# A modulated transformer block on one core: one load moved ahead, gates ahead of LoRA parts, one moment on another engine, two banks traded, two FFN steps reordered

## The chip, the cores and the metric

One core of one Trainium2 chip runs the whole program in one launch. The metric is the device time in microseconds (us); lower is better. The engines are named as in the profile: PE is the tensor engine, DVE the vector engine, ACT the scalar engine, POOL the GpSimd engine, and SPq is the queue of the sync engine, which here issues nearly all DMAs.

## The reference

Two batches of 512 tokens with 512 features go through a block with adaptive layer norm: six modulation vectors (a shift, a scale and a gate for each half) come from `silu(c) @ wmod`.

```python
mod = (_silu(L0_c) @ L0_wmod).reshape(2, 6, 1, -1)
sa, ca, ga, sb, cb, gb = (mod[:, 0], mod[:, 1], mod[:, 2], mod[:, 3], mod[:, 4], mod[:, 5])
ga = (2 * (ga >= 0) - 1) * jnp.maximum(jnp.abs(ga), 0.25)      # gb likewise
h = _layernorm(x) * (1 + ca) + sa
x = x + ga * (h @ (weight * mask_by_32x32_blocks).T + bias)      # first half
h = _layernorm(x) * (1 + cb) + sb
h1 = lora(h, w1, A1, B1); h3 = lora(h, w3, A3, B3)               # hidden width 1376, rank 16, scaling 2
x = x + gb * lora(silu(h1) * h3, w2, A2, B2)                     # the FFN
```

## The kernel before

Every product is computed in about fp32 accuracy with three passes in fp32r: each operand is split in a high part and a low part, and high x high, high x low and low x high are added up in PSUM. ACT mostly makes the high parts (a copy with a cast) and DVE the low parts (source minus high).

There is no scheduler. Each engine runs its own hand-written list of instructions in order, and semaphores tie the lists together. So an instruction that waits holds up all that stands behind it in its engine's list. The same holds for the list of DMAs that SPq issues; they all go over one set of DMA engines.

The first half works as follows. PE builds scale columns from `ca`; the layer norm is folded into the masked weight and four rank-one terms, so that `attend(b, k, m, tiles)` can multiply raw x by scaled weights for batch b, block k of the features and pass m. What the norm still needs comes in by `attend_end(b)`, which multiplies two small tiles: `norm_rows` (the moments of x, turned by PE in `turn_moments(b)`) and `uv_parts` (the masked weight times shift and scale, from `rows_sa`, `columns_sa`, `uv`, `uv_select`, and split by DVE in `uv_split`). The moments of batch 0 are DVE's `moment_a(0, t)` (two instructions, statistics and aggregation), and those of batch 1 are ACT's `row_sum`, `means` and `square_sum`; POOL takes the root of each in `root(i, at)`. The gate `ga` comes from PE `gate_rows(0)`, ACT `gate_abs(0)`, DVE `gates_of(0)`, PE `spread_gate`, and an ACT copy. `turn_moments(0)` may not overwrite the bank `up_b` before `gates_of(0)` has read it (it waits for `gates_ready`).

Then DVE multiplies each tile of batch 0 by gate and norm (`attn_gate`), POOL and DVE add two tiles each to x (`add_x1`), DVE takes the moments of the new x (`moment_f(i)`), POOL takes their roots in two calls of two tiles, ACT and DVE normalize two tiles each (`norm`), and PE turns the result (`turn(q)`, into banks `up_a`, `up_b` and the two side banks); ACT's `high(q)` puts in shift and scale and makes the high part.

The FFN walks over 22 steps s (11 blocks j of the hidden width for each batch): `up(s, 0)` into `up_a`, `up(s, 1)` into `up_b`, then `down(s - 1, t)`. The LoRA terms are merged into the weights while batch 0 runs. A weight comes in three pieces for each j (PIECE numbers them): for a piece, PE `merge(r)` multiplies LoRA parts into a bank, DVE `merge(r)` adds it to the loaded weight, ACT `weight_high(r)` makes its high part and DVE `weight_low(r)` its low part. LoRA tensors themselves come in five cuts, each made into a high part by ACT `lora_high(n)` and completed by DVE `lora_part(n)`; `parts_ready` counts the latter. POOL `spread(j)` makes the small tile b13 for the merges from the first parts. The first two merges use `up_a` and `up_b`, before `turn(0)` and `turn(1)` write there.

Of the kernel before, what the change touches and what calls it, by code (L numbers as in the profile page):

```python
# [9 lines left out]
ACT = mybir.ActivationFunctionType  # L10
# [11 lines left out]
T = S // P  # L22
# [106 lines left out]
def build(nc, x, x_cols, mask, weight, bias, ffn, lora, c, wmod_ca, wmod_sa, wmod, identity, consts, out):  # L129
# [4 lines left out]
    with ExitStack() as ctx:  # L134
# [165 lines left out]
        stats_ready = [sem(f"stats_ready{i}") for i in range(4)]  # L300
        moments_ready = [sem(f"moments_ready{i}") for i in range(4)]
# [84 lines left out]
        def merge_bank(r):  # L386
            return (up_b, up_a)[r] if r < FIRST_MERGES else side[SIDE[("merge", r)] % 2]
# [33 lines left out]
        def _(sp):  # L421

            def load_x(b):
                for t in range(T):
                    sp.dma_start(xt[:, b, t], x_rows[b, :, t]).then_inc(x_loaded[b][t], 16)
# [22 lines left out]
            load_x(0)  # L448
            load_x_chunk(1, 0)
            sp.dma_start(sa_sb[:], wmod_sa).then_inc(sa_loaded, 16)  # L450
            for k in range(1, KT):
                load_x_chunk(1, k)
            load_lora(0)
            load_lora(1)
            load_mod(GATE_A, SHIFT_F, wmod_ga_loaded)
            load_x(1)
# [29 lines left out]
        def _(pool):  # L486
# [6 lines left out]
            def root(i, at):  # L493
# [6 lines left out]
                else:  # L500
                    pool.wait_ge(moments_ready[i], n)
# [76 lines left out]
        def _(act):  # L578
# [57 lines left out]

            def norm_rows_evacuate(b):
# [83 lines left out]
            lora_high(0)  # L721
            lora_high(1)
            gate_abs(0)
            row_sum(0)
            row_sum(1)
            norm_rows_evacuate(0)
            uv_high()
            row_sum(2)

            act.wait_ge(gate_spread, 1)  # L730
            nc.scalar.activation(gate_row_a[0], up_b[:], ACT.Copy).then_inc(gate_copied, 1)
            row_sum(3)
# [3 lines left out]
            mod_evacuate()  # L736
            norm(0)
# [39 lines left out]
        def _(dve):  # L777
# [225 lines left out]
            moment_a(0, 0)  # L1003
            moment_a(0, 1)
            masked_weight_low(1, 1)
            moment_a(0, 2)
            columns_sa()
            moment_a(0, 3)
            masked_weight_low(1, 2)
            norm_parts(0)  # L1010
            uv_sum()
            lora_part(0)
            gates_of(0)
            masked_weight_low(1, 3)
            lora_part(1)
            uv_split()
            nc.vector.tensor_copy(half_on[:], const[:, HALF_ON:HALF_ON + 2]).then_inc(half_on_ready, 1)
# [16 lines left out]
            moment_f(3)  # L1034
            merge(0)
            norm_parts(1)
# [503 lines left out]
```

## Time and profile before

| | us |
|---|---|
| median of 3 runs | 253.34 (253.24 to 253.77) |
| the profiled execution | 253.32 |
| its span in the trace | 251.5 |
| PE busy in the span | 240.4 |
| DVE, ACT, POOL busy | 150.8, 92.4, 41.5 |

The span is that of the engines' instructions; 1.8 us of the profiled execution's time lie outside it. The PE stream is continuous for nearly all of the span, so the table is read by its complement: the span less PE's busy time, 11.1 us, is all that a change in the order of work can touch at all.

### The profile page before, as it was taken

The numbers are of one execution on the slowest core, as the hardware profiler recorded it, in microseconds if no ns is written. First come the engines' busy times: TensorE is split into PE (matmuls) and PEld (weight loads), VectorE is DVE, ScalarE is ACT, GpSimd is POOL, SyncE is SP. The second block draws the span as 40 slices with busy tenths as digits, with TensorE's granted clock in tenths as the row PEclk, the third lists the DMA queues.
The fourth block names the chain that finished last, engine by engine and source line by source line (L and its number), as shares of the span: only waits on it lengthen the run. The fifth ranks groups of instructions, "written<-read, shape, count | busy, mean of one in ns | idle before, by whom it ended". The sixth has DMA issues, their size and how long they took to land.

```text
span 251.5 us, 3419 instructions
## 1 busy us (share of the span) xinstructions
PE 240.4 (96%) x1205; PEld 187.7 (75%) x1205; DVE 150.8 (60%) x260; ACT 92.4 (37%) x168; POOL 41.5 (16%) x57
## 2 busy tenths in 40 slices
PE   7998979799899999999999999999999999999993
PEld 5666546576688888888888878888888888888772
DVE  2769499889886787854654525536453345334524
ACT  2364565673552332375465313112221122122210
POOL 2002367503210130430330100160000000000000
PEclk9999999999999999999999999999999999999999
DMA  5999999322041413133213751040000000000004
GB/s 139 367 389 397 394 402 373 80 86 72 23 175 66 122 46 101 51 102 124 84 44 119 43 42 9 1 167 3 0 1 0 0 3 0 0 0 3 0 0 167
DMA packets 14565, 26.37 MB, mean 105 GB/s; under 512 B 1618, under 2 KB 3538, under 8 KB 14420
## 3 DMA queue, kind: packets, MB, share of 16 engines
q1 hardware_dynamic: 14112, 26.01, 33.2%
q8 instruction: 10, 0.16, 0.3%
q10 hardware_dynamic: 436, 0.15, 0.2%
q14 instruction: 7, 0.06, 0.1%
HBM read 23.26 MB, written 2.10 MB: 101 GB/s over the span
## 4 chain that ended last, share of the span: by engine, by line
PE 77%; DVE 9%; DMA 5%; SPq 4%; issue 3%; POOL 1%; ACT 0%; DVEq 0%; POOLq 0%
PE up_a L1319 16%; PE up_b L1319 15%; PE acc L1345 8%; PE acc L1347 8%; PE acc L1346 8%; PE up_a L1328 8%; PE up_b L1328 7%; DMA sa_sb<-in_wmod_sa 5%; PE side L1301 2%; DVE parts L920 1%; PE acc L1273 1%; DVE wa L933 1%; DVE raw L949 1%; DVE xt L979 1%; PE side L1306 1%
## 5 line engine op out<-in xcount | busy, mean ns | idle before, releaser
L1073 DVE TENSOR_TENSOR g<-up_b,g 128x512 f32<-128x512 f32 (+1 forms) x22 | 15.2, 689 | 43.6 <-PE up_b L1328 43.6
L1345 PE MATMUL acc<-w_hi,g_hi 128*128 128x512 f32 (+1 forms) x88 | 34.9, 396 | 0.0
L1347 PE MATMUL acc<-w_hi,g_lo 128*128 128x512 f32 (+1 forms) x88 | 34.8, 395 | 0.0
L1346 PE MATMUL acc<-w_lo,g_hi 128*128 128x512 f32 (+1 forms) x88 | 34.7, 395 | 0.0
L764 ACT ACTIVATE g_hi<-g 128x512 fp32r<-128x512 f32 (+1 forms) x22 | 13.9, 632 | 54.3 <-DVE g L1073 54.3
L949 DVE SCALAR_TENSOR_TENSOR raw<-side,raw 128x512 f32<-128x512 f32 (+2 forms) x31 | 20.2, 677 | 19.3 <-PE side L1301 11.8
L696 ACT ACTIVATE w_hi<-raw 128x512 fp32r<-128x512 f32 (+2 forms) x33 | 20.3, 626 | 16.0 <-DVE raw L949 16.0
L754 ACT ACTIVATE g<-up_a 128x512 f32<-128x512 f32 (+1 forms) x22 | 13.1, 595 | 32.8 <-PE up_a L1328 32.8
L1319 PE MATMUL up_a<-ht_hi,w_hi 128*128 128x512 f32 (+1 forms) x88 | 24.5, 400 | 0.0
L1319 PE MATMUL up_a<-ht_hi,w_lo 128*128 128x512 f32 (+1 forms) x88 | 23.9, 393 | 0.6 <-DVE w_lo L955 0.6
L1319 PE MATMUL up_b<-ht_hi,w_hi 128*128 128x512 f32 (+1 forms) x88 | 24.0, 394 | 0.0
L1328 PE MATMUL up_b<-ht_lo,w_hi 128*128 128x512 f32 (+1 forms) x88 | 23.8, 392 | 0.0
L1328 PE MATMUL up_a<-ht_lo,w_hi 128*128 128x512 f32 (+1 forms) x88 | 23.8, 392 | 0.0
L1319 PE MATMUL up_b<-ht_hi,w_lo 128*128 128x512 f32 (+1 forms) x88 | 23.7, 391 | 0.0
L955 DVE TENSOR_TENSOR w_lo<-raw,w_hi 128x512 fp32r<-128x512 f32 (+2 forms) x33 | 21.6, 680 | 2.4 <-ACT w_hi L696 0.7
L1077 DVE TENSOR_TENSOR g_lo<-g,g_hi 128x512 fp32r<-128x512 f32 (+1 forms) x22 | 15.1, 688 | 8.6 <-ACT g_hi L764 8.4
L530 POOL TENSOR_SCALAR b<-parts,half_on 128x128 fp32r<-128x128 f32 (+1 forms) x22 | 14.9, 689 | 32.2 <-PE side L1301 19.0
L1319 PEld LDWEIGHTS up_a<-ht_hi,w_lo 128*128 128x128 f32 (+1 forms) x88 | 16.2, 186 | 5.0 <-DVE w_lo L955 1.0
L1345 PEld LDWEIGHTS acc<-w_hi,g_hi 128*128 128x128 f32 (+1 forms) x88 | 16.5, 188 | 4.1 <-issue 0.2
L1347 PEld LDWEIGHTS acc<-w_hi,g_lo 128*128 128x128 f32 (+1 forms) x88 | 16.5, 188 | 4.0
L1346 PEld LDWEIGHTS acc<-w_lo,g_hi 128*128 128x128 f32 (+1 forms) x88 | 16.5, 188 | 3.9
L1319 PEld LDWEIGHTS up_b<-ht_hi,w_lo 128*128 128x128 f32 (+1 forms) x88 | 16.3, 185 | 3.9
(156 smaller groups left out, 339.8 us busy)
## 6 DMA issues: line engine op xcount, KB each, us to landing
raw<-in_ffn SPq DMA_DIRECT2D x33, 256.0 KB, 2.7
xt<-in_x SPq DMA_DIRECT2D x8, 256.0 KB, 9.1
wmod_sb<-in_wmod SPq DMA_DIRECT2D x2, 1024.0 KB, 12.8
wmod_sb<-in_wmod SPq DMA_DIRECT2D x1, 2048.0 KB, 14.7
out<-xt SPq DMA_DIRECT2D x8, 256.0 KB, 2.5
mask_sb<-in_mask SPq DMA_DIRECT2D x4, 256.0 KB, 6.2
ca_sb<-in_wmod_ca SPq DMA_DIRECT2D x4, 256.0 KB, 6.2
wa<-in_weight SPq DMA_DIRECT2D x4, 256.0 KB, 6.4
```

Of the source, the lines that this page charges most:

```text
L530: nc.gpsimd.tensor_scalar(b13[:, n, 0:w], f32(parts[:, LORA_B13 + j * P:LORA_B13 + j * P + w]), half_on[:, n:n + 1], None, ALU.mult).then_ ...
L696: nc.scalar.activation(dst, src, ACT.Copy).then_inc(w_high_ready, 1)
L764: nc.scalar.activation(g_hi[s % 2][0:w], g[0:w], ACT.Copy).then_inc(g_high_ready, 1)
L949: nc.vector.scalar_tensor_tensor(w, merge_bank(r)[0:rows, 0:cols], SCALING, w, ALU.mult, ALU.add).then_inc(merged, 1)
L955: nc.vector.tensor_tensor(low_part, src, f32(high), ALU.subtract).then_inc(w_ready, 1)
L1073: nc.vector.tensor_tensor(g[0:w], up_b[0:w], g[0:w], ALU.mult).then_inc(g_ready, 1)
L1077: nc.vector.tensor_tensor(g_lo[s % 2][0:w], g[0:w], f32(g_hi[s % 2][0:w]), ALU.subtract).then_inc(g_low_ready, 1)
L1319: nc.tensor.matmul(dst[0:w], w_part[j][:, k, n], ht_hi[b][:, k], start=(m == 0 and k == 0), stop=False)
L1328: last = nc.tensor.matmul(dst[0:w], up_hi[j][:, k, n], ht_lo[b][:, k], start=False, stop=(k == KT - 1))
L1345: nc.tensor.matmul(acc[t][:], hi, down_hi[j][0:w], start=(j == 0), stop=False)
L1346: nc.tensor.matmul(acc[t][:], hi, down_lo[j][0:w], start=False, stop=False)
L1347: last = nc.tensor.matmul(acc[t][:], lo, down_hi[j][0:w], start=False, stop=(j == HT - 1))
```

## The change

Nothing of the arithmetic changes but the way in which one tile's mean and variance are computed. In the order of the program:

- SPq: the load of `sa_sb` (1 MB) goes ahead of x tiles 1 to 3 of batch 0; the load of the first gate's weights (`wmod_sb`, 1 MB) goes ahead of two LoRA cuts, and these go between x tiles 1 and 2 of batch 1.
- DVE: `columns_sa` moves behind `moment_a(0, 3)`; `gates_of(0)` and `uv_split` move ahead of `lora_part(0)`. ACT: the two `lora_high` move behind `uv_high` and `norm_rows_evacuate(0)`, which change places, and `row_sum(2)` moves behind the copy of the gate.
- The moments of the last tile of batch 0 after the first half: DVE's `moment_f(3)` goes, ACT's new `moment_last()` comes (a sum, two tiny scalings, a sum of squares), and POOL's root waits for it.
- The first merges trade banks (`up_a` first), each `turn(q)` waits for its own bank's merge alone, PE issues `merge(0)` ahead of the `attend(1, 2, ...)` block, and DVE does `norm_parts(1)` ahead of its `merge(0)`.
- FFN steps 0 and 1 on DVE: `lora_part(2)` goes ahead of everything, `attn_gate(1, 1)` to `(1, 3)` go from between the merges to the ends of steps 0 and 1, `gates_of(1)` goes behind the product of h1 and h3, and `lora_part(4)` goes into the middle piece of step 2.

```diff
@@ def merge_bank
-            return (up_b, up_a)[r] if r < FIRST_MERGES else side[SIDE[("merge", r)] % 2]
+            return (up_a, up_b)[r] if r < FIRST_MERGES else side[SIDE[("merge", r)] % 2]
@@ POOL root
-                    pool.wait_ge(moments_ready[i], n)
+                    if i == NORM_F[0] and n == T:
+
+                        pool.wait_ge(moments_ready[i], T - 1)
+                        pool.wait_ge(last_summed, 4)
+                    else:
+                        pool.wait_ge(moments_ready[i], n)
@@ ACT
+            def moment_last():
+
+                i, t = NORM_F[0], ORDER[T - 1]
+                act.wait_ge(*x1_done(T - 1))
+                act.wait_ge(moments_ready[NORM_A[1]], T + 1)
+                nc.scalar.activation(hbuf[:, 0], xt[:, 0, t], ACT.Copy, accum_out=total[:, 0:1]
+                                     ).then_inc(last_summed, 1)
+                act.wait_ge(last_summed, 1)
+                nc.scalar.activation(total[:, 1:2], total[:, 0:1], ACT.Copy, scale=-D ** -1.5
+                                     ).then_inc(last_summed, 1)
+                nc.scalar.activation(moments[:, i, T - 1, 0:1], total[:, 0:1], ACT.Copy, scale=1.0 / D
+                                     ).then_inc(last_summed, 1)
+                act.wait_ge(last_summed, 3)
+                nc.scalar.activation(hbuf[:, 1], xt[:, 0, t], ACT.Square, bias=total[:, 1:2],
+                                     scale=D ** -0.5, accum_out=moments[:, i, T - 1, 1:2]
+                                     ).then_inc(last_summed, 1)
...
-            lora_high(0)
-            lora_high(1)
             gate_abs(0)
             row_sum(0)
             row_sum(1)
+            uv_high()
             norm_rows_evacuate(0)
-            uv_high()
-            row_sum(2)
+            lora_high(0)
+            lora_high(1)
 
             act.wait_ge(gate_spread, 1)
             nc.scalar.activation(gate_row_a[0], up_b[:], ACT.Copy).then_inc(gate_copied, 1)
+            row_sum(2)
             row_sum(3)
...
             mod_evacuate()
+            moment_last()
             norm(0)
@@ DVE
-            moment_f(3)
+            norm_parts(1)
             merge(0)
-            norm_parts(1)
             norm(0, 2, ORDER[2])
             norm(0, 3, ORDER[3])
             merge(1)
...
-            for i in range(2):
-                attn_gate(1, i)
+            lora_part(2)
+            attn_gate(1, 0)
             for s in range(B * HT):
...
-                if s < 2:
-                    lora_part(2 + s)
+                if s == 1:
+                    lora_part(3)
...
-                if s == 0:
-                    gates_of(1)
-                    for i in range(2, T):
-                        attn_gate(1, i)
-                if s == 2:
-                    lora_part(4)
                 if piece_mid(s):
                     merge(PIECE[piece_mid(s)])
+                    lora_part(4)
                     weight_low(PIECE[piece_mid(s)])
...
+                if s == 0:
+                    gates_of(1)
...
+                if s < 2:
+                    for i in ((1,), (2, 3))[s]:
+                        attn_gate(1, i)
@@ PE
-                if q == 0:
-
-                    pe.wait_ge(merged, FIRST_MERGES)
+                if q < FIRST_MERGES:
+
+                    pe.wait_ge(merged, q + 1)
...
                 if r == 0:
 
+                    pe.wait_ge(uv_ready, 1)
+                elif r == 1:
+
                     pe.wait_ge(cols_ready, 1)
-                elif r == 1:
-
-                    pe.wait_ge(uv_ready, 1)
...
             columns_f()
+            pe.wait_ge(parts_ready, 2)
+            merge(0)
             for m in range(3):
                 attend(1, 2, m, last_two)
-            pe.wait_ge(parts_ready, 2)
-            merge(0)
             attend(1, 3, 0, last_two)
```

The list of DMAs on SPq, from the last of the loads that stay where they were, with what goes and what comes (`xt` is x by tiles, `raw<-in_x_cols` is x of batch 1 by features, `wmod_sb` with 4x512 is the first gate, with 4x1024 the shift and scale of the FFN):

```order
-L425 DMA xt<-in_x 128x512 x4
+L425 DMA xt<-in_x 128x512
 L428 DMA raw<-in_x_cols 128x512
 L450 DMA sa_sb<-in_wmod_sa 128x2048
+L425 DMA xt<-in_x 128x512 x3
 L428 DMA raw<-in_x_cols 128x512 x3
+L437 DMA wmod_sb<-in_wmod 128x4x512
+L425 DMA xt<-in_x 128x512 x2
 L434 DMA lora_raw<-in_lora 128x256
 L434 DMA lora_raw<-in_lora 128x640
-L437 DMA wmod_sb<-in_wmod 128x4x512
-L425 DMA xt<-in_x 128x512 x4
```

The 1 MB of `sa_sb` now has one x tile ahead of it where it had four, and the first gate's 1 MB has none of the LoRA cuts ahead of it; the two x tiles that the piece ends with come behind the cuts.

DVE's list in the first half, before, from `columns_sa` (L861) on; L789 and L791 are a moment, L819 to L826 `norm_parts(0)`, L898 the sum for uv, L920 a `lora_part`, L909 and L912 `gates_of(0)`, L891 the low part of a masked weight:

```order
L861 COPY uv_cols<-up_b 128x4x2 [waits sa_cols_out]
L789 BN_STATS stats<-xt 128x6 [waits moments_ready0,x_loaded0_3]
L791 BN_AGGR moments<-stats 128x2 [waits stats_ready0]
L891 SCALAR_TENSOR_TENSOR wa_lo<-wa,uv_cols,wa_hi 128x512 [waits wa_high_ready1]
L819 SCALAR_TENSOR_TENSOR moments<-moments,rstd 128x4 [waits norm_cols_cleared,rstd_ready0]
L823 CAST norm_cols<-moments 128x4x2x2 [waits deviation_ready]
L826 TENSOR_TENSOR norm_cols<-moments,norm_cols 128x4x2 [waits norm_high_ready]
L898 TENSOR_TENSOR g<-up_a,gate_row 128x512 [waits bias_loaded,uv_out]
L920 SCALAR_TENSOR_TENSOR parts<-parts,const,lora_raw 128x256 [waits const_loaded,parts_high_ready]
L909 TENSOR_SCALAR block_ones<-up_b 128x128 [waits gate_abs_ready]
L912 SCALAR_TENSOR_TENSOR block_ones<-mod_rows,block_ones 128x128 [waits gate_sign_ready]
L891 SCALAR_TENSOR_TENSOR wa_lo<-wa,uv_cols,wa_hi 128x512 [waits wa_high_ready1]
```

The same place in the changed kernel, from the small copy `half_on` on; L888 is now `columns_sa`, L846 to L853 `norm_parts(0)`, L936 and L939 `gates_of(0)`, L918 the low part, L930 `uv_split` and L947 the two `lora_part`:

```order
L1037 COPY half_on<-const 128x2 [waits const_loaded]
L888 COPY uv_cols<-up_b 128x4x2 [waits sa_cols_out]
L846 SCALAR_TENSOR_TENSOR moments<-moments,rstd 128x4 [waits norm_cols_cleared,rstd_ready0]
L850 CAST norm_cols<-moments 128x4x2x2 [waits deviation_ready]
L853 TENSOR_TENSOR norm_cols<-moments,norm_cols 128x4x2 [waits norm_high_ready]
L925 TENSOR_TENSOR g<-up_a,gate_row 128x512 [waits bias_loaded,uv_out]
L936 TENSOR_SCALAR block_ones<-up_b 128x128 [waits gate_abs_ready]
L939 SCALAR_TENSOR_TENSOR block_ones<-mod_rows,block_ones 128x128 [waits gate_sign_ready]
L918 SCALAR_TENSOR_TENSOR wa_lo<-wa,uv_cols,wa_hi 128x512 [waits wa_high_ready1]
L930 SCALAR_TENSOR_TENSOR uv_parts<-uv_parts,const,up_a 128x512 [waits const_loaded,uv_high_ready]
L947 SCALAR_TENSOR_TENSOR parts<-parts,const,lora_raw 128x256 [waits const_loaded,parts_high_ready]
L947 SCALAR_TENSOR_TENSOR parts<-parts,const,lora_raw 128x640 [waits const_loaded,parts_high_ready]
```

The moment that stood behind `columns_sa` is now ahead of it, and the gates stand directly behind the sum for uv, with both LoRA parts at the end.

DVE's list at the start of the FFN, before; L933 is `attn_gate`, L949 `merge`, L920 `lora_part(2)`, L955 `weight_low`, L909 and L912 `gates_of(1)`, L1073 the product of h1 and h3, L1077 its low part:

```order
L933 SCALAR_TENSOR_TENSOR wa<-acc,rstd,mask_sb 128x512 [waits gate_row_loaded0_1,x1_by_pool,rstd_ready2,attn_out] x2
L949 SCALAR_TENSOR_TENSOR raw<-side,raw 128x512 [waits merge_out,raw_loaded2]
L949 SCALAR_TENSOR_TENSOR raw<-side,raw 128x512 [waits merge_out,raw_loaded3]
L920 SCALAR_TENSOR_TENSOR parts<-parts,const,ca_sb 128x1120 [waits const_loaded,parts_high_ready]
L955 TENSOR_TENSOR w_lo<-raw,w_hi 128x512 [waits w_high_ready] x2
L909 TENSOR_SCALAR gates_f<-side 128x128 [waits gate_abs_ready]
L912 SCALAR_TENSOR_TENSOR gates_f<-mod_rows,gates_f 128x128 [waits gate_sign_ready]
L933 SCALAR_TENSOR_TENSOR wa<-acc,rstd,mask_sb 128x512 [waits gate_row_loaded0_1,x1_by_dve,rstd_ready2,attn_out] x2
L1073 TENSOR_TENSOR g<-up_b,g 128x512 [waits h3_out,silu_ready]
L1077 TENSOR_TENSOR g_lo<-g,g_hi 128x512 [waits g_high_ready]
```

The same place in the changed kernel, where L947 is `lora_part(2)`, L960 `attn_gate`, L976 `merge`, L982 `weight_low`, L1095 the product and L1101 its low part:

```order
L947 SCALAR_TENSOR_TENSOR parts<-parts,const,ca_sb 128x1120 [waits const_loaded,parts_high_ready]
L960 SCALAR_TENSOR_TENSOR wa<-acc,rstd,mask_sb 128x512 [waits gate_row_loaded0_1,x1_by_pool,rstd_ready2,attn_out]
L976 SCALAR_TENSOR_TENSOR raw<-side,raw 128x512 [waits merge_out,raw_loaded2]
L976 SCALAR_TENSOR_TENSOR raw<-side,raw 128x512 [waits merge_out,raw_loaded3]
L982 TENSOR_TENSOR w_lo<-raw,w_hi 128x512 [waits w_high_ready] x2
L1095 TENSOR_TENSOR g<-up_b,g 128x512 [waits h3_out,silu_ready]
L936 TENSOR_SCALAR gates_f<-side 128x128 [waits gate_abs_ready]
L939 SCALAR_TENSOR_TENSOR gates_f<-mod_rows,gates_f 128x128 [waits gate_sign_ready]
L1101 TENSOR_TENSOR g_lo<-g,g_hi 128x512 [waits g_high_ready]
L960 SCALAR_TENSOR_TENSOR wa<-acc,rstd,mask_sb 128x512 [waits gate_row_loaded0_1,x1_by_pool,rstd_ready2,attn_out]
```

The low parts of the first FFN weights follow the merges directly; the LoRA part that stood between them is ahead, and three of four `attn_gate` are behind.

## Rows read from the trace of the kernel before

**Rows 1.** The page's busy times, and windows: length, busy per engine, clock, DMA.

```profile
PE 240.4 (96%) x1205; PEld 187.7 (75%) x1205; DVE 150.8 (60%) x260; ACT 92.4 (37%) x168; POOL 41.5 (16%) x57
...
9.20:24.00 14.80, 13.67 (x84) 9.62 (x88) 11.94 (x26) 7.64 (x14) 1.27 (x1) 1.00 1.05 393
...
80.00:251.50 171.50, 167.70 (x749) 135.44 (x747) 88.84 (x141) 52.13 (x92) 19.60 (x24) 1.00 0.19 45
```

**Rows 2.** PE's timeline, idle spans: start, length, instruction, [idle before, releaser].

```profile
23.88 1.08 PE L1165 MATMUL up_b<-sa_sb,silu_c 128*32 128x128 f32 x32 [1.13 <-DMA sa_sb<-in_wmod_sa]
...
33.76 0.62 PE L1201 MATMUL up_b<-ident,norm_cols 128*108 128x128 f32 x4 [1.28 <-DVE block_ones L912]
...
47.29 0.65 PE L1201 MATMUL side<-ident,norm_cols 128*108 128x128 f32 x4 [0.43 <-DVE norm_cols L826]
49.04 0.63 PE L1131 MATMUL up_a<-ident,work 128*128 128x128 f32 x4 [1.10 <-DVE raw L949]
...
60.91 1.19 PE L1319 MATMUL up_a<-ht_hi,w_lo 128*128 128x512 f32 x4 [0.58 <-DVE w_lo L955]
...
67.23 0.47 PE L1306 MATMUL side<-parts 128*128 128x512 f32 x1 [0.84 <-DVE parts L920]
```

**Rows 3.** PE's timeline, steps of the stream between those waits.

```profile
22.12 0.63 PE L1273 MATMUL acc<-wa_hi,ht_lo 128*128 128x512 f32 x2
...
29.81 1.08 PE L1235 MATMUL up_b<-wmod_sb,silu_c 128*32 128x128 f32 x32
...
40.30 1.93 PE L1213 MATMUL up_b<-wmod_sb,silu_c 128*32 128x256 f32 x32
...
51.81 1.23 PE L1319 MATMUL up_a<-ht_hi,w_hi 128*128 128x512 f32 x4
...
59.17 1.16 PE L1319 MATMUL up_a<-ht_hi,w_hi 128*128 128x512 f32 x4
```

**Rows 4.** DVE's timeline, from the last moment of batch 0 to `add_x1(0, 2)`.

```profile
27.26 0.69 DVE L789 BATCH_NORM_STATS2 stats<-xt 128x6 f32<-128x512 f32 x1
...
32.58 1.03 DVE L912 SCALAR_TENSOR_TENSOR block_ones<-mod_rows,block_ones 128x128 f32<-128x128 f32 x1
33.54 1.75 DVE L891 SCALAR_TENSOR_TENSOR wa_lo<-wa,uv_cols,wa_hi 128x512 fp32r<-128x512 f32 x1
35.22 0.87 DVE L920 SCALAR_TENSOR_TENSOR parts<-parts,const,lora_raw 128x640 fp32r<-128x640 f32 x1
...
37.40 1.41 DVE L933 SCALAR_TENSOR_TENSOR wa<-acc,rstd,mask_sb 128x512 f32<-128x512 f32 x2 [0.55 <-PE acc L1282]
...
40.04 1.29 DVE L939 TENSOR_TENSOR xt<-wa,xt 128x512 f32<-128x512 f32 x1
```

**Rows 5.** POOL's timeline: `x_low(1)` to `x_low(3)`, and the second root's start.

```profile
30.78 3.96 POOL L511 TENSOR_TENSOR ht_lo<-raw,ht_hi 128x512 fp32r<-128x512 f32 x3 [0.70 <-DVE norm_cols L826]
...
46.10 0.23 POOL L502 TENSOR_SCALAR rstd<-moments 128x2 f32<-128x2 f32 x1 [1.28 <-DVE moments L791]
```

**Rows 6.** DMA: `sa_sb` in the chain; issue of `wmod_sb`, and its time to landing.

```profile
12.20 11.64 DMA sa_sb<-in_wmod_sa
...
22.86 0.43 SPq L437 DMA_DIRECT2D wmod_sb<-in_wmod  x1
...
wmod_sb<-in_wmod SPq DMA_DIRECT2D x1, 2048.0 KB, 14.7
```

**Rows 7.** ACT's timeline: a sum of squares, `high(0)`, two `weight_high`.

```profile
40.03 0.71 ACT L634 ACTIVATE hbuf<-xt,total 128x512 f32<-128x512 f32 x1
...
49.71 0.78 ACT L662 ACTIVATE ht_hi<-up_a,shift,one_plus 128x512 fp32r<-128x512 f32 x1
...
57.80 1.23 ACT L696 ACTIVATE w_hi<-raw 128x512 fp32r<-128x512 f32 x2 [0.44 <-DVE raw L949]
```

**Rows 8.** DVE's timeline at the start of the FFN: two merges, `lora_part(2)`.

```profile
57.07 1.29 DVE L949 SCALAR_TENSOR_TENSOR raw<-side,raw 128x512 f32<-128x512 f32 x2 [0.43 <-PE side L1301]
58.28 1.37 DVE L920 SCALAR_TENSOR_TENSOR parts<-parts,const,ca_sb 128x1120 fp32r<-128x1120 f32 x1
```

More of the change, by code:

```diff
@@ L300, in build @@
         stats_ready = [sem(f"stats_ready{i}") for i in range(4)]
+        last_summed = sem("last_summed")
         moments_ready = [sem(f"moments_ready{i}") for i in range(4)]
@@ L421, in _, with load_x @@
         def _(sp):
-            def load_x(b):
-                for t in range(T):
-                    sp.dma_start(xt[:, b, t], x_rows[b, :, t]).then_inc(x_loaded[b][t], 16)
+            def load_x(b, t):
+                sp.dma_start(xt[:, b, t], x_rows[b, :, t]).then_inc(x_loaded[b][t], 16)
             def load_x_chunk(b, k):
@@ L447, in _ @@
                 load_x_chunk(0, k)
-            load_x(0)
+            load_x(0, 0)
             load_x_chunk(1, 0)
             sp.dma_start(sa_sb[:], wmod_sa).then_inc(sa_loaded, 16)
+            for t in range(1, T):
+                load_x(0, t)
             for k in range(1, KT):
                 load_x_chunk(1, k)
-            load_lora(0)
-            load_lora(1)
             load_mod(GATE_A, SHIFT_F, wmod_ga_loaded)
-            load_x(1)
+            for t in range(T):
+                if t == 2:
+                    load_lora(0)
+                    load_lora(1)
+                load_x(1, t)
             load_mod(SHIFT_F, GATE_F, wmod_f_loaded)
@@ L1003, in _ @@
             moment_a(0, 0)
+            masked_weight_low(1, 1)
             moment_a(0, 1)
-            masked_weight_low(1, 1)
             moment_a(0, 2)
-            columns_sa()
             moment_a(0, 3)
             masked_weight_low(1, 2)
+            dve.wait_ge(const_loaded, 16)
+            nc.vector.tensor_copy(half_on[:], const[:, HALF_ON:HALF_ON + 2]).then_inc(half_on_ready, 1)
+            columns_sa()
             norm_parts(0)
             uv_sum()
-            lora_part(0)
             gates_of(0)
             masked_weight_low(1, 3)
+            uv_split()
+            lora_part(0)
             lora_part(1)
-            uv_split()
-            nc.vector.tensor_copy(half_on[:], const[:, HALF_ON:HALF_ON + 2]).then_inc(half_on_ready, 1)
             dve.wait_ge(norm_rows_out, 1)
```

## The prediction

> **What bounds the kernel now.** I read the page first, then PE's own timeline, then for each idle span in it the engine named as its releaser. PE is busy for 240.4 of 251.5 us, and from 80 us on for 167.7 of 171.5, at a granted clock of 1.00 (2.4 GHz) [rows 1]. So behind 80 us only the tail (some 3.8 us in which DVE and the stores finish) is not PE, and nothing of the change is there. The table is decided by six idle spans of PE between 22 and 68 us [rows 2]: 1.13 (the load of `sa_sb`), 1.28 (`gates_of(0)`), 0.43 (`norm_parts(1)`), 1.10 (`merge(1)`), 0.58 (`weight_low` of the second FFN block) and 0.84 (`lora_part(3)`). Their sum is 5.36 us, and it is nearly the most that any reordering can give, as PE's own list keeps its work.
>
> A second bound lies under them. Up to about 38 us the DMA engines are saturated (393 GB/s and a share of 1.05 from 9 to 24 us [rows 1]). The load of the FFN's shift and scale, 2 MB, is issued at 22.86 and lands 14.7 us later, at 37.6 [rows 6]. The change puts the same bytes ahead of it, so it lands at 37.6 again. PE needs it for `mod_rows_f`, which starts at 40.30 now [rows 3]. Before that point PE can't gain more than 2.7 us.
>
> **The change part by part**, as start times of PE's steps, before and after.
>
> *The load of sa.* Three x tiles, 0.79 MB, leave the queue ahead of it: 0.79 MB at 393 GB/s is 2.0 us. It landed at 12.20 + 11.64 = 23.84 [rows 6], so now at about 21.8. PE's stream reaches `rows_sa` at 22.12 + 0.63 = 22.75 [rows 3]. So the 1.13 goes, with 0.9 us to spare: 23.88 becomes 22.75. What is late next: the x tiles land behind sa, the third at 21.8 + 2.0 = 23.8, and DVE, which went through two of the four moments before it had to wait for `columns_sa`, gets to the last at about 24.9. They are in time, and no longer stand behind `columns_sa` (the last started at 27.26 [rows 4], now about 25). The first gate's weights land 0.46 MB / 393 = 1.2 us earlier; PE came to them at 29.81 [rows 3] and comes now at 28.68. I count nothing there; it is a tie.
>
> *The gates.* `turn_moments(0)` waited for L912, which ran from 32.58 to 33.61 [rows 4]. Ahead of it stood norm parts (which waited for the root of the last moment), the uv sum and `lora_part(0)`. With the moment 2.2 us earlier and the LoRA part behind, the root is done near 27.7, the uv sum by 28.8, and the gates then wait for PE's `gate_rows(0)` itself, plus ACT: about 30.1. L912 is 0.3 us of work, but reads two SBUF tiles, and while POOL's three `x_low` passes (1.32 us each) ran from 30.78 to 34.74 it took 1.03, and the L891 behind it 1.75, ending 0.55 after POOL's last pass [rows 4, 5]. POOL starts these passes right after `norm_parts(0)`, so now at 28.2, with ends near 29.5, 30.8 and 32.2. So L912 waits for 30.8 and ends near 31.0. PE comes at 33.76 - 1.13 - 1.28 = 31.35 [rows 2]. The 1.28 goes. (The Trainium skill, SBUF — State Buffer, section "Who interferes with whom", calls this an exclusive lock on a port pair: a DVE instruction with two SBUF inputs and a GpSimd instruction that reads SBUF block each other for a whole instruction. The trace agrees in the 1.03 and 1.75. Without such a rule L912 would be done at 30.4, and PE would come at 31.35 all the same, so the sum is the same by both.)
>
> *To mod_rows_f.* `uv_split`, behind the delayed L891 (until about 32.8), is done at 33.5; PE's `attend_end(0)` needs it near 34.2. Fine. So `mod_rows_f` starts at 40.30 - 2.41 = 37.9, 0.3 us behind its DMA. Gain so far 2.4.
>
> *The chain to turn(0).* `attn_gate(0, 0)` started at 37.40 [rows 4]. Now DVE has `uv_split` to 33.5, `lora_part(0)` 0.35 and `lora_part(1)` 0.87 (the row's) ahead of it, and PE's and ACT's results are there by 34.5: start 34.8, 2.6 earlier. Four gates at 0.67 [rows 4] end at 37.5; POOL's two adds end near 38.4, and `add_x1(0, 2)`, another instruction with two SBUF inputs (1.29 beside POOL [rows 4]), ends near 38.9, the second add 1.4 later at 40.3. Then ACT's `moment_last`: two passes of 0.71 [rows 7], each with an accumulator read of 0.1 to 0.2, and two tiny ones of 0.2, so 1.9 us, to 42.2. ACT is free: from the gate's copy, done at 34.4, it has two sums and four squares at 0.7 and 0.4 for the means, so its batch 1 sums end near 39.0; `mod_evacuate` ends near 40.2. POOL's second root therefore starts near 42.4 where it started at 46.10 [rows 5], and is done at 43.5. In place of the moment and with `norm_parts(1)` first, DVE is through `merge(0)` at 43.8 and its two norms at 44.9. `turn(0)` no longer waits for `merge(1)`. PE's stream could start it at 49.04 - 1.10 - 0.43 - 2.41 = 45.1 [rows 2]. Both say 45.1: gain 3.9.
>
> *Where some is given back.* ACT's `high(q)` stands behind `weight_high(1)`, which waits for `merge(1)` (to 45.5): `high(0)` starts near 46.2, against 49.71 [rows 7], a gain of 3.5. The first FFN product, 51.81 [rows 3], would come at 47.9 and needs the fourth `high`, done at 46.2 + 2.8 = 49.0, for its fourth matmul, due at 48.6: 0.4 back. Gain 3.5. (That moving PE's `merge(0)` costs nothing follows from `spread(0)`, done near 35.8, against a start of 41.3.)
>
> *FFN steps 0 and 1.* DVE ends its batch 0 low parts near 51.7, waits for ACT's LoRA part until 52.0, and takes `lora_part(2)`, 1.3 of 1.37 [rows 8], and one `attn_gate`: the merges start at 54.0 (57.07 [rows 8]), ACT's two high parts end 1.96 later as before (57.07 to 57.80 + 1.23 = 59.03 [rows 7]) at 56.0. PE would come at 59.17 - 3.5 = 55.7 [rows 3] and so waits 0.35 for a high part. It then starts the product with low parts at 57.0, and these are ready at 56.7. That is against 60.91 [rows 2]: gain 3.9. `lora_part(3)` ends near 61.8, and PE's late merge comes at 67.23 - 3.9 - 0.84 = 62.5 [rows 2]: gain 4.8. Step 2 is the tightest left: `weight_low` of the middle piece is ready about 0.1 us before PE wants it, as DVE now has two gates more in front. Behind it the order is as before.
>
> **The sum:** 1.13 + 1.28 + 0.43 + 1.10 + 0.58 + 0.84 = 5.36, less 0.35 to 0.45 that stays behind `high` and some 0.2 behind the high part: 4.8 us. The profiled execution took 253.32, 0.02 from the median, so 248.5.
>
> **Rivals.**
> - *All of it.* If the waits for `high(3)` and for the high part don't show, 5.4 to 5.8 (idle spans are listed with modelled matmul ends, which hides up to 0.16 us in each): 247.6.
> - *A port or a queue gives some back.* POOL's `spread(0)` becomes ready in the very moment in which DVE goes from `lora_part(0)` to `lora_part(1)`. If POOL is first, DVE waits 0.6 a pass, and `attn_gate(0, 0)` and everything to `turn(0)` is 0.6 to 1.2 late: 249.1 to 249.7. Likewise sa, if it is held by the slowest of the DMA engines and not by the bytes ahead: up to 1.1 back, 249.6. And the step 2 piece: 0.3 to 0.7 if DVE is late. Two of these make 250.3. For it: L891's 1.75 shows how dear one such meeting is. Against: each has its own slack.
> - *The change doesn't do what it says.* The spans vanish, and the last of them takes all: if DVE, not PE, bounds steps 0 to 2, the FFN starts at the old time. DVE goes from the merges to `lora_part(2)` without a pause now [rows 8], but the changed order has the same work there, and it starts 3.5 us earlier. 253.0 to 253.7.
> - *Slower: x tiles late.* The three x tiles of batch 0 now come behind sa, and DVE's list waits for each with the low part of a masked weight, `columns_sa` and all else behind. It decides from the point where tile 3 lands after 24.9; to eat the gain it must land after 24.9 + 4.8 = 29.7. At 393 GB/s it lands at 23.8. If it were at 30.5: 254.1. Nothing in the trace speaks for this.
>
> **How the numbers follow.** The forecast with "all of it" 0.66 (247.6 to 249.0), the partial case 0.25 (249.0 to 251.5), no effect 0.04, slower 0.05. To leave out 2 in 10 the range goes from 247.6 to 250.3; the likeliest case's own is 248.0 to 249.0. A measurement tells 0.2% (0.5 us) from no change: faster 0.91, within 0.04, slower 0.05.
>
> **What would show it.** `rows_sa` at 22.7 with no idle; `turn_moments(0)` near 31.3; `mod_rows_f` near 37.9, never before 37.6; POOL's second root near 42.4; `turn(0)` near 45.1; a new idle of some 0.4 for `high` in the first FFN product and of some 0.3 for a high part at 56; the late merge near 62.4 with no idle; the end 4.8 earlier. The prediction is wrong if L912 or `lora_part(1)` sits behind a POOL pass longer than 0.3, if `mod_rows_f` names a DMA, or if PE waits for `weight_low` in step 2.

## The result and the profile after

The changed kernel takes 249.2 us (249.14 to 249.43, 4 runs) against 253.52 of the kernel before (253.24 to 253.77, 4 runs): a ratio of 0.983 with a 95% interval of 0.9815 to 0.985, 4.3 us faster. The forecast was 248.5 in a range of 247.6 to 250.3, so the direction was right and the size 0.7 us too good. The span went from 251.5 to 247.4. Of the runs of the kernel before that stand beside experiments 6, 7, 8 and 10, two of 19 took 256.3 against 253.1 to 254.0 of the others; this widens the intervals of those ratios and draws them down (the medians alone give 0.996 for experiment 7 and 0.994 for experiment 8).

The page of the profile after begins as follows (busy us, share, instructions).

```profile
PE 239.4 (97%) x1205; PEld 187.3 (76%) x1205; DVE 150.2 (61%) x258; ACT 94.6 (38%) x174; POOL 40.6 (16%) x57
```

PE does the same 1205 instructions. Its idle time fell from 11.1 to 8.0 us, and its busy time by 1.0 as well. Of this, 0.6 is the row of 12 matmuls at the very start (5.05 us before, 4.48 after, with 0.75 of idle behind it), which the change doesn't touch. These are PE's own rows after that answer to [rows 2] and [rows 3], with start, length, and idle before it with its releaser.

```profile
6.67 0.37 PE L1283 MATMUL up_a<-mask_part,block_ones 128*128 128x16 f32 x2 [0.75 <-DVE mask_part L901]
...
22.89 1.08 PE L1192 MATMUL up_b<-sa_sb,silu_c 128*32 128x128 f32 x32
...
27.71 1.06 PE L1208 MATMUL up_a<-wa,uv_cols 128*32 128x512 f32 x8 [0.63 <-DVE uv_cols L888]
...
32.32 0.62 PE L1228 MATMUL up_b<-ident,norm_cols 128*108 128x128 f32 x4 [0.35 <-DVE block_ones L939]
...
38.67 1.93 PE L1240 MATMUL up_b<-wmod_sb,silu_c 128*32 128x256 f32 x32
...
45.94 0.66 PE L1158 MATMUL up_a<-ident,work 128*128 128x128 f32 x4 [0.28 <-DVE work L828]
...
48.96 1.42 PE L1346 MATMUL up_a<-ht_hi,w_hi 128*128 128x512 f32 x4
...
56.96 1.17 PE L1346 MATMUL up_a<-ht_hi,w_hi 128*128 128x512 f32 x4 [0.27 <-ACT w_hi L722]
57.97 1.07 PE L1346 MATMUL up_a<-ht_hi,w_lo 128*128 128x512 f32 x4
...
63.03 0.40 PE L1333 MATMUL side<-parts 128*128 128x512 f32 x1
```

The spans for sa, `norm_parts(1)`, `merge(1)`, `weight_low` and `lora_part(3)` are gone. A new one of 0.63 stands in front of `uv` (L1208), and 0.35 of the gates' 1.28 is left. A wait of 0.28 for a norm at `turn(0)` and one of 0.27 for a high part in FFN step 1 are new. As start times:

| PE step | before | forecast | after |
|---|---|---|---|
| `rows_sa` | 23.88 | 22.75 | 22.89 |
| `turn_moments(0)` | 33.76 | 31.35 | 32.32 |
| `mod_rows_f` | 40.30 | 37.9 | 38.67 |
| `turn(0)` | 49.04 | 45.1 | 45.94 |
| product with low parts, step 1 | 60.91 | 57.0 | 57.97 |
| late merge, step 1 | 67.23 | 62.5 | 63.03 |

The loss against the forecast is all there by `turn_moments(0)` (0.97 us) and is smaller at the late merge (0.5). So I looked at DVE between 22 and 33 us. These are its rows after, with POOL's in the same stretch under them.

```profile
22.07 0.69 DVE L816 BATCH_NORM_STATS2 stats<-xt 128x6 f32<-128x512 f32 x1
22.80 0.18 DVE L818 BATCH_NORM_AGGREGATE moments<-stats 128x2 f32<-128x6 f32 x1
22.89 1.55 DVE L918 SCALAR_TENSOR_TENSOR wa_lo<-wa,uv_cols,wa_hi 128x512 fp32r<-128x512 f32 x1
24.37 0.68 DVE L816 BATCH_NORM_STATS2 stats<-xt 128x6 f32<-128x512 f32 x1
...
25.99 0.67 DVE L816 BATCH_NORM_STATS2 stats<-xt 128x6 f32<-128x512 f32 x1
...
26.79 0.72 DVE L918 SCALAR_TENSOR_TENSOR wa_lo<-wa,uv_cols,wa_hi 128x512 fp32r<-128x512 f32 x1
...
27.50 0.16 DVE L888 COPY uv_cols<-up_b 128x8 f32<-128x8 f32 x1
...
31.16 1.01 DVE L939 SCALAR_TENSOR_TENSOR block_ones<-mod_rows,block_ones 128x128 f32<-128x128 f32 x1
...
22.61 1.29 POOL L520 TENSOR_TENSOR ht_lo<-raw,ht_hi 128x512 fp32r<-128x512 f32 x1 [20.46 <-ACT ht_hi L616]
...
29.51 3.79 POOL L520 TENSOR_TENSOR ht_lo<-raw,ht_hi 128x512 fp32r<-128x512 f32 x3 [0.69 <-DVE norm_cols L853]
```

The same stretch before, where the low part is L891:

```profile
22.69 0.66 DVE L789 BATCH_NORM_STATS2 stats<-xt 128x6 f32<-128x512 f32 x1
...
23.48 0.73 DVE L891 SCALAR_TENSOR_TENSOR wa_lo<-wa,uv_cols,wa_hi 128x512 fp32r<-128x512 f32 x1
24.14 0.68 DVE L789 BATCH_NORM_STATS2 stats<-xt 128x6 f32<-128x512 f32 x1
...
22.40 1.27 POOL L511 TENSOR_TENSOR ht_lo<-raw,ht_hi 128x512 fp32r<-128x512 f32 x1 [20.25 <-ACT ht_hi L607]
```

The low part of the masked weight (L918) at 22.89 takes 1.55 us, and the same instruction at 26.79 takes 0.72. POOL's first `x_low` pass runs from 22.61 to 23.90, and the slow L918 ends at 24.44, 0.54 behind it. Before, two moments stood ahead of this low part, and it met only the last 0.2 us of the pass. The change also trades it with the second of them, a pair of lines that stands neither in the description of the change nor in the prediction. So it now starts 0.3 us into POOL's pass. Everything behind it in DVE's list is 0.8 us late: `columns_sa` (L888) at 27.50, for which PE waits 0.63, and the last moment at 25.99 where I had about 25.

### The profile page after: what moved, and what is told of

It reads as the page before. It is cut to its first block, busy times and chain, and to the rows that moved or that the text cites. A ratio compares the mean times of both kernels' runs of the same rounds, so it can differ in the third digit from the quotient of the medians.

```text
span 247.4 us, 3423 instructions
## 1 busy us (share of the span) xinstructions
PE 239.4 (97%) x1205; PEld 187.3 (76%) x1205; DVE 150.2 (61%) x258; ACT 94.6 (38%) x174; POOL 40.6 (16%) x57
## 4 chain that ended last, share of the span: by engine, by line
PE 84%; DVE 8%; DMA 2%; issue 1%; ACT 1%; POOL 0%; SPq 0%; DVEq 0%; POOLq 0%; ACTq 0%
PE up_a L1346 17%; PE up_b L1346 16%; PE acc L1372 8%; PE up_a L1355 8%; PE acc L1374 8%; PE acc L1373 8%; PE up_b L1355 8%; PE acc L1300 3%; DMA wa<-in_weight 2%; PE side L1328 2%; DVE stats L816 2%; PE side L1300 2%; DVE wa_lo L918 1%; DVE xt L1006 1%; PE side L1333 1%
## 5 line engine op out<-in xcount | busy, mean ns | idle before, releaser
L1095 DVE TENSOR_TENSOR g<-up_b,g 128x512 f32<-128x512 f32 (+1 forms) x22 | 15.2, 690 | 43.2 <-PE up_b L1355 43.2
L791 ACT ACTIVATE g_hi<-g 128x512 fp32r<-128x512 f32 (+1 forms) x22 | 13.9, 632 | 51.2 <-DVE g L1095 51.2
L976 DVE SCALAR_TENSOR_TENSOR raw<-side,raw 128x512 f32<-128x512 f32 (+2 forms) x31 | 20.2, 677 | 19.1 <-PE side L1328 11.4
L982 DVE TENSOR_TENSOR w_lo<-raw,w_hi 128x512 fp32r<-128x512 f32 (+2 forms) x33 | 21.6, 681 | 1.8
L1101 DVE TENSOR_TENSOR g_lo<-g,g_hi 128x512 fp32r<-128x512 f32 (+1 forms) x22 | 15.1, 688 | 8.1 <-ACT g_hi L791 7.9
L539 POOL TENSOR_SCALAR b<-parts,half_on 128x128 fp32r<-128x128 f32 (+1 forms) x22 | 14.4, 665 | 31.3 <-PE side L1328 29.1
L1346 PEld LDWEIGHTS up_a<-ht_hi,w_hi 128*128 128x128 f32 (+1 forms) x88 | 15.9, 186 | 4.5 <-issue 0.5
## 6 DMA issues: line engine op xcount, KB each, us to landing
wmod_sb<-in_wmod SPq DMA_DIRECT2D x1, 2048.0 KB, 14.6
```

The costliest lines, as they stand in the source:

```text
L539: nc.gpsimd.tensor_scalar(b13[:, n, 0:w], f32(parts[:, LORA_B13 + j * P:LORA_B13 + j * P + w]), half_on[:, n:n + 1], None, ALU.mult).then_ ...
L791: nc.scalar.activation(g_hi[s % 2][0:w], g[0:w], ACT.Copy).then_inc(g_high_ready, 1)
L976: nc.vector.scalar_tensor_tensor(w, merge_bank(r)[0:rows, 0:cols], SCALING, w, ALU.mult, ALU.add).then_inc(merged, 1)
L982: nc.vector.tensor_tensor(low_part, src, f32(high), ALU.subtract).then_inc(w_ready, 1)
L1095: nc.vector.tensor_tensor(g[0:w], up_b[0:w], g[0:w], ALU.mult).then_inc(g_ready, 1)
L1101: nc.vector.tensor_tensor(g_lo[s % 2][0:w], g[0:w], f32(g_hi[s % 2][0:w]), ALU.subtract).then_inc(g_low_ready, 1)
```

## Experiments

All times are medians, and each ratio is to runs of the kernel before taken beside that experiment, with medians of 253.31 to 253.55. The changed kernel itself ran beside experiments 9, 11 and 12 only. Its eight runs, there and in the result, took 249.09 to 249.43.

**1. The low part behind the second moment again.**

```diff
             moment_a(0, 0)
-            masked_weight_low(1, 1)
             moment_a(0, 1)
+            masked_weight_low(1, 1)
             moment_a(0, 2)
```

> The changed kernel with one pair of DVE's list put back: the low part of the masked weight (batch 1, block 1) stands behind the second moment of batch 0 again, not ahead of it. Theory A (the two-input DVE instruction met POOL's first x_low pass, took 1.55 us in place of 0.72, and all of DVE's list behind it is 0.8 us late): that instruction is back at 0.7 to 0.9, columns_sa comes 0.6 earlier, PE's wait of 0.63 for it falls under 0.1, and the time is 0.4 to 0.7 below the changed kernel, 248.5 to 248.8. Theory B (the x tiles, landing behind sa, or the first gate's load set the pace there): the second moment waits for its tile, and the time stays at 249.2 or is above it.

Measured: 248.74 (248.22 to 249.08), ratio to before 0.982 (0.9805 to 0.983). DVE's row:

```profile
23.52 0.75 DVE L918 SCALAR_TENSOR_TENSOR wa_lo<-wa,uv_cols,wa_hi 128x512 fp32r<-128x512 f32 x1
```

0.75 instead of 1.55; `columns_sa` starts at 26.52, and PE's wait for it is gone. This is theory A. The second moment started at 22.72 without a wait, so the x tile was there. The five runs lie just below those of the changed kernel, edge to edge.

**2. `columns_sa` right behind the last moment.** As experiment 1, and:

```diff
             moment_a(0, 3)
+            columns_sa()
             masked_weight_low(1, 2)
...
-            columns_sa()
             norm_parts(0)
```

> As low_later, and columns_sa stands directly behind the last moment, ahead of the low part of block 2 and the small copy. Theory A, carried on: uv starts as soon as PE gets there, with no wait at all, and the low part is done in the shadow of POOL's root; a further 0 to 0.3 us, 248.3 to 248.7. Theory B: no difference from the changed kernel, 249.2.

Measured: 248.42 (248.26 to 248.49), ratio 0.980 (0.979 to 0.9815). The median is 0.3 below experiment 1, but the two ranges overlap, so this further step is not shown apart.

**3. POOL alone changed, DVE's list as in the changed kernel.** This takes the order of the list out of the question.

```diff
             pool.wait_ge(exponent_ready, 1)
+            pool.wait_ge(wa_low_ready[1], 2)
             x_low(0)
```

> The changed kernel with DVE's list untouched; POOL alone is changed: it starts its first x_low pass only when the low part of the masked weight that it met (batch 1, block 1) is done. If the meeting of the two instructions is the cause, and not the order of DVE's list as such, the low part is back at about 0.75, the last moment starts near 25.2, PE waits for columns_sa under 0.1, and the time is that of low_later: 248.4 to 248.8. If the cause lies in the list (the x tile, the order), it stays at 249.2. If the later x_low pass is itself needed sooner than 25 us, the time is above 249.2.

Measured: 248.42 (248.32 to 248.89), ratio 0.9805 (0.979 to 0.982). DVE's and POOL's rows there:

```profile
22.82 0.72 DVE L919 SCALAR_TENSOR_TENSOR wa_lo<-wa,uv_cols,wa_hi 128x512 fp32r<-128x512 f32 x1
...
25.08 0.68 DVE L817 BATCH_NORM_STATS2 stats<-xt 128x6 f32<-128x512 f32 x1
...
23.68 1.29 POOL L520 TENSOR_TENSOR ht_lo<-raw,ht_hi 128x512 fp32r<-128x512 f32 x1 [21.53 <-DVE wa_lo L919]
```

With the same instruction in the same place of the same list, and POOL's pass out of its way, it takes 0.72. The meeting is the cause. The last moment starts at 25.1, as the prediction had it, PE no longer waits for `columns_sa`, and the time is 0.1 from the forecast.

**4. POOL's later passes behind the gates.** As experiment 1, and:

```diff
             for k in range(1, KT):
+                if k == 2:
+                    pool.wait_ge(gates_ready, 1)
                 x_low(k)
```

> As low_later, and POOL takes its third and fourth x_low pass only when the gates are ready, so that the gates' two-input instruction meets no pass but the first of the three. If the meeting with POOL sets when turn_moments(0) starts, that instruction falls from 1.0 to about 0.3 us and turn_moments(0) shows no wait; 0 to 0.3 us below low_later. Rival: the passes come later and now hit the low part behind the gates or make PE wait for x_low: equal to low_later or 0.3 to 0.8 above it.

Measured: 248.73 (248.46 to 249.06), the same as experiment 1. The gates' instruction does fall to 0.29, and PE no longer waits for it, but the time moves on:

```profile
30.54 0.29 DVE L941 SCALAR_TENSOR_TENSOR block_ones<-mod_rows,block_ones 128x128 f32<-128x128 f32 x1
30.75 0.74 DVE L920 SCALAR_TENSOR_TENSOR wa_lo<-wa,uv_cols,wa_hi 128x512 fp32r<-128x512 f32 x1
...
32.81 2.14 DVE L949 SCALAR_TENSOR_TENSOR parts<-parts,const,lora_raw 128x256 fp32r<-128x256 f32 x2
...
30.91 2.96 POOL L520 TENSOR_TENSOR ht_lo<-raw,ht_hi 128x512 fp32r<-128x512 f32 x2 [0.82 <-DVE block_ones L941]
```

The two LoRA parts now meet the passes (2.14 us for both, against 1.27 in experiment 1), DVE's `attn_gate` starts no sooner (34.91 against 34.81), and PE waits 0.46 at `turn(0)`. The rival held in its time. But the passes hit the LoRA parts and not the low part (L920), which started 0.16 ahead of them.

**5. The load of sa put back behind the x tiles**, in the changed kernel.

```diff
-            load_x(0, 0)
+            for t in range(T):
+                load_x(0, t)
             load_x_chunk(1, 0)
             sp.dma_start(sa_sb[:], wmod_sa).then_inc(sa_loaded, 16)
-            for t in range(1, T):
-                load_x(0, t)
```

> The changed kernel with the load of sa behind the four x tiles again, all else as changed. If the load is worth its span: PE waits 1.1 us for it at rows_sa as before, later waits shrink by what was slack (0.6 at uv, 0.3 at the gates), and the time is 0.3 to 1.1 above the changed kernel, 249.5 to 250.3. Rival, that DVE's list alone made the gain: 249.2.

Measured: 249.31 (249.11 to 249.49). This is below the range of 249.5 to 250.3 and nearer to the rival, 0.1 above the changed kernel and not told apart from it. PE's wait for the load is back in full:

```profile
24.37 1.08 PE L1191 MATMUL up_b<-sa_sb,silu_c 128*32 128x128 f32 x32 [1.41 <-DMA sa_sb<-in_wmod_sa]
...
27.66 0.17 DVE L887 COPY uv_cols<-up_b 128x8 f32<-128x8 f32 x1
...
31.93 0.29 DVE L938 SCALAR_TENSOR_TENSOR block_ones<-mod_rows,block_ones 128x128 f32<-128x128 f32 x1
```

and yet nearly nothing is lost. `rows_sa` is 1.5 late against the changed kernel, `uv` 0.8 (28.49), `turn_moments(0)` 0.3 (32.59) and `turn(0)` 0.2 (46.15). Two places take the delay up. DVE does `columns_sa` at 27.66, where it did it at 27.50 without the wait: DVE, late behind the slow low part, was the bound there. And the gates' instruction, which took 1.01 from 31.16 beside POOL, comes at 31.93 here, takes 0.29 and ends at the same 32.2.

**6. The same edit with DVE repaired** (experiment 2 with sa behind the tiles).

> cols_first with the load of sa behind the four x tiles again. If the load was worth nothing in the changed kernel only because DVE's list was late there for another reason (the low part that met POOL), it is worth its 1.1 to 1.4 us of wait here, less slack: 0.5 to 1.1 above cols_first, 248.9 to 249.5. Rival: 0 to 0.2 above cols_first, as in the changed kernel.

Measured: 249.48 (249.28 to 249.69), 1.06 above experiment 2, where the kernels before that ran beside them differ by 0.13. The idle is 1.08:

```profile
23.89 1.08 PE L1191 MATMUL up_b<-sa_sb,silu_c 128*32 128x128 f32 x32 [1.08 <-DMA sa_sb<-in_wmod_sa]
```

So the load's move is worth its whole span where DVE is in time, and 0.1 in the kernel that was made. Experiments 1 and 3 give the missing 0.7 us back, and 5 and 6 together show why the load seemed to be worth nothing: of two edits of the same place, one hid the other.

**7. The load of sa alone**, in the kernel before.

```diff
-            def load_x(b):
-                for t in range(T):
+            def load_x(b, ts=range(T)):
+                for t in ts:
...
-            load_x(0)
+            load_x(0, range(1))
             load_x_chunk(1, 0)
             sp.dma_start(sa_sb[:], wmod_sa).then_inc(sa_loaded, 16)
+            load_x(0, range(1, T))
```

> The kernel before with one edit: the load of sa goes ahead of x tiles 1 to 3 of batch 0. If a span of PE is worth its length wherever the next waits hang on it: columns_sa comes 1.1 earlier and with it the last moment, the root and the gates, so 1.0 to 1.2 us below before, 252.1 to 252.4. Rival (putting the load back cost the changed kernel only 0.1, so it is worth little anywhere): 253.1 to 253.5.

Measured: 252.43 (252.26 to 252.78) against 253.55, ratio 0.994 (0.991 to 0.998). The load is worth its span of 1.13 here. DVE's chain came about 1.0 earlier as expected (`columns_sa` at 26.14, 27.17 before). But PE's rows hold something that I had not expected:

```profile
30.05 1.08 PE L1236 MATMUL up_b<-wmod_sb,silu_c 128*32 128x128 f32 x32 [1.36 <-DMA wmod_sb<-in_wmod]
```

The first gate's weights, issued at 16.84, landed at 30.0, and PE waited for them. This wait took the place of the 1.28 for `gates_of(0)`, which is gone: PE now comes to `turn_moments(0)` at 32.74, and the gates end at 32.60. In the changed kernel, where the second edit of the load order puts this load ahead of the LoRA cuts, it is issued at 13.72, landed at 28.8, and PE starts `gate_rows(0)` at 29.38 with no wait. How much of the gates' gain hangs on this second edit is not shown, since no run undoes it alone.

**8. The FFN's DVE order alone**, in the kernel before (all parts of the diff for DVE in the section on the change but the first).

> The kernel before with the changed order of DVE's FFN steps 0 to 2 alone. By the prediction's terms (0.58 and 0.84, less some 0.3 for a high part): 1.0 to 1.3 us below before, 252.1 to 252.5. Rival (DVE bounds these steps whatever its order): 253.3.

Measured: 252.08 (251.67 to 252.4) against 253.55, ratio 0.992 (0.989 to 0.995): 1.5 us, or 1.4 with the two runs of 256.3 left out, somewhat more than expected. PE's rows:

```profile
59.44 1.17 PE L1319 MATMUL up_a<-ht_hi,w_hi 128*128 128x512 f32 x4 [0.27 <-ACT w_hi L696]
60.45 1.08 PE L1319 MATMUL up_a<-ht_hi,w_lo 128*128 128x512 f32 x4
...
65.51 0.39 PE L1306 MATMUL side<-parts 128*128 128x512 f32 x1
```

The late merge comes at 65.51 instead of 67.23 [rows 2], 1.7 earlier, of which 0.2 was there before the FFN (`turn(0)` at 48.85 instead of 49.04).

**9. The FFN's DVE order put back**, in the changed kernel (the reverse of that edit).

> The changed kernel with DVE's FFN steps 0 to 2 in the order of before. If the parts add up: 1.0 to 1.3 us above the changed kernel, 250.2 to 250.5. Rival: the earlier start of the FFN makes the old order better or worse than before, so a difference outside 0.7 to 1.6.

Measured: 250.69 (250.51 to 251.1); the changed kernel beside it 249.2. This is 1.5 us again, more than the 1.0 to 1.3 expected: the part adds up with the others. PE waits for `weight_low` and `lora_part(3)` as before:

```profile
58.26 1.20 PE L1346 MATMUL up_a<-ht_hi,w_lo 128*128 128x512 f32 x4 [0.57 <-DVE w_lo L982]
...
64.57 0.47 PE L1333 MATMUL side<-parts 128*128 128x512 f32 x1 [0.84 <-DVE parts L947]
```

**10. The last moment on DVE again**, in the changed kernel.

```diff
             columns_f()
             centres()
+            moment_f(3)
             norm_parts(1)
@@ ACT
-            moment_last()
@@ POOL root
-                    if i == NORM_F[0] and n == T:
-
-                        pool.wait_ge(moments_ready[i], T - 1)
-                        pool.wait_ge(last_summed, 4)
-                    else:
-                        pool.wait_ge(moments_ready[i], n)
+                    pool.wait_ge(moments_ready[i], n)
```

> The changed kernel with the last moment on DVE again, behind centres, and POOL's root waiting for it. POOL's second root then starts near 44.6 in place of 43.4, DVE's norms and turn(0) come 1.0 to 1.2 later: 250.0 to 250.4. Rival (PE's stream, not the moment, sets turn(0)): at most 0.3 above the changed kernel.

Measured: 250.33 (250.17 to 251.12), 1.1 above the changed kernel. POOL's second root and PE's `turn(0)`:

```profile
44.81 0.23 POOL L506 TENSOR_SCALAR rstd<-moments 128x2 f32<-128x2 f32 x1 [1.29 <-DVE moments L812]
...
47.08 0.66 PE L1153 MATMUL up_a<-ident,work 128*128 128x128 f32 x4 [1.03 <-DVE work L822]
```

**11. `turn(0)` waits for both merges**, in the changed kernel.

```diff
-                    pe.wait_ge(merged, q + 1)
+                    pe.wait_ge(merged, FIRST_MERGES)
```

> The changed kernel, where turn(0) waits for both first merges as before. turn(0) itself comes 0.6 later (46.5), but ACT's high(0) is held by weight_high(1) until 47.05 anyway, so by the theory that ACT sets the next step the time rises by 0 to 0.2: 249.2 to 249.4. Rival, that turn(0) is on the path: 0.5 to 0.6 above, 249.7 to 249.8.

Measured: 249.4 (249.21 to 249.77), against 249.2 of the changed kernel beside it. `turn(0)` comes at 46.46, 0.5 late, but the next step on the way is ACT's:

```profile
46.35 0.63 ACT L722 ACTIVATE w_hi<-raw 128x512 fp32r<-128x512 f32 x1 [0.22 <-DVE raw L976]
47.13 0.78 ACT L688 ACTIVATE ht_hi<-up_a,shift,one_plus 128x512 fp32r<-128x512 f32 x1
```

In the changed kernel `high(0)` starts at 47.05, here at 47.13, in a profile that is 0.16 ahead at `uv` (27.55). That 0.1 to 0.2 is all, and it is inside the runs' spread.

**12. The changed kernel once more.**

> The changed kernel once more, unedited, beside the two others of this call, to set the scale on this chip: 249.2, within 0.3. In its profile the low part beside POOL's first x_low pass takes 1.5 us again if the meeting is a property of the order and not of one execution.

Measured: 249.2 (249.09 to 249.24). The low part beside POOL takes 1.55 again, and PE waits 0.65 for `columns_sa`.

## Why the prediction was right, and where it was off

*What bounds the kernel: right.* Five of six spans are gone from PE and the sixth is 0.35; behind 70 us PE's rows only stand 4.15 to 4.3 us earlier. The spans' sum was a fair bound. It seems that they hide a little more than they show, as the rival "all of it" said: the FFN's two spans of 0.58 and 0.84 with 0.27 left behind would be 1.15, and experiments 8 and 9 measured 1.4 to 1.5.

*The load of sa: mechanism right, worth less.* It landed at 20.6 (issued at 10.37, 10.2 us) where I had 21.8; `rows_sa` had no wait. The step that failed is the next one: "DVE [...] gets to the last at about 24.9". It got there at 25.99, because the low part of the masked weight, put ahead of the second moment, met POOL's pass and took 1.55 instead of 0.72. I had weighed just such meetings for L912 and for `lora_part(1)`, but priced the low part at its undisturbed time in its new place. The reading of the old list was off too: three of the four moments, not two, were done when DVE waited for `columns_sa` (the third at 24.14). Experiments 1 and 3 return 0.5 and 0.8 us, two ways, and arrive at 248.7 and 248.4, about the forecast.

*The range: in part luck.* The likeliest case (247.6 to 249.0) was just missed. 249.2 lies in the partial one, to which the prediction gave 0.25 ("a port or a queue gives some back", 249.1 to 249.7 for one meeting). That rival had the right kind of meeting in the wrong place: the two LoRA parts beside POOL's `spread(0)` took 1.27, about the 1.22 that the forecast has for them without a meeting.

*The gates: right in the main.* L939, the L912 of before, took 1.01 as before, since POOL's three passes and the gates moved together, and it ended at 32.17 where the forecast had 31.0. Of PE's 1.28 there, 0.35 is left, which the sum put at nothing. With DVE's list in time it is 0.24 (experiment 1), 0.17 (3) and none (2), so not all of it was DVE's lateness. The sign of being wrong, "L912 [...] sits behind a POOL pass longer than 0.3", came by its letter (1.01 against 0.29 undisturbed), but the working itself had L912 wait for a pass, so it was a poor sign. (The Trainium skill, SBUF — State Buffer, section "Who interferes with whom", calls the port pair that VectorE and GpSimd share an exclusive lock, says that a vector instruction with two SBUF inputs contends there with a GpSimd instruction that reads SBUF, and that the order of issue decides who waits. The runs agree: the low part took 1.55 with POOL's pass under way, and in experiment 4, where it started 0.16 ahead of POOL, it took 0.74, and POOL's two passes took 2.96 in place of some 2.5.)

*The first gate's load: a tie, as forecast.* The load landed at 28.8 and PE came at 29.38. In experiments 1 to 3 PE comes at 28.50 to 28.84, the row of its weight load names this DMA, and PE's row shows no idle.

*mod_rows_f: the floor is there.* It starts at 38.67 in the changed kernel, and its load (issued at 23.28, 14.6 to landing) was there at 37.9. With DVE's list in time it starts at 37.70, 37.93 and 37.76 (experiments 1 to 3), and the row of its weight load (PEld) names the DMA, as in experiment 1:

```profile
37.69 1.45 PEld L1240 LDWEIGHTS up_b<-wmod_sb,silu_c 128*32 128x32 f32 x32 [0.36 <-DMA wmod_sb<-in_wmod]
```

The changed kernel has 0.37 of idle in the same row with no DMA named, so this costs nothing yet. But the second bound of the prediction is reached there: what comes sooner ahead of this step would gain nothing more without this load.

*moment_last and the banks: right in place.* ACT's pass from 41.28 to 43.18 is the 1.9 of the sum, and POOL's second root follows at 43.37, 1.0 behind the forecast, as `turn_moments(0)` is. Worth 1.1 (experiment 10). The single-bank wait is worth 0 to 0.2 (experiment 11), since ACT's `high(0)` stands behind `weight_high(1)`; the prediction gave 0.4 back there for `high`, and the row of the first FFN product shows 0.2 (1.42 against 1.23).

*FFN steps 0 to 2: right.* PE waits 0.27 for the high part (0.35 forecast), the late merge has no wait, and the middle piece of step 2 is just in time: DVE's last low part ends at 72.48, and PE starts its first product at 72.63.

What stays open: 0.1 to 0.2 us of the lateness at the first steps comes from the start of the program (PE's wait of 0.75 at 6.67), where the change has nothing. Such waits of 0.3 to 0.8 come and go between the profiles (none in experiment 1, 0.45 in experiment 2), and single start times carry 0.1 to 0.3 of uncertainty by them.

## What to carry to other kernels

When an instruction is moved, price it in its new place with what the other engine does there: here a vector instruction with two SBUF inputs, started with 1.0 us of a GpSimd pass left, cost 0.8 more, and next to nothing with 0.2 left. An idle span that goes away gives its length only if no other list was just as late behind it. Undoing a single edit showed 0.1 us here for an edit that is worth 1.1, so try it in a kernel where the second cause is repaired as well. Moving the wait to the engine that can afford it (one line on POOL, 248.42) did as well as reordering the list (248.74 and 248.42).

## What the runs showed of the hardware

The low part of the masked weight, a DVE instruction with two SBUF inputs of 128x512, took 1.55 us when it started 0.28 into a POOL pass of 1.29, and ended 0.54 behind it. It took 0.72 with no pass beside it, and 0.73 to 0.75 with 0.2 us of the pass left (before and experiment 1).

DVE gets in between two back-to-back POOL passes, and so waits for one and not for three: L939 at 31.16 ended at 32.17 with POOL's three passes running from 29.51 to 33.30. It is so in the kernel before too, and I had used it, from [rows 4, 5].

Not expected was how early the 1 MB load came: with 0.79 MB fewer ahead it landed 3.2 us sooner (23.84 to 20.6), and its issue was 1.8 sooner (12.20 to 10.37), while 0.79 MB at 393 GB/s is only 2.0. What made the rest is open.
